# A four-layer attention and expert kernel: constants ahead of the last sends, first rows rounded in halves, the dense expert by 512 columns

## What is computed

```python
topv, topi = jax.lax.top_k(logits, TOP_K)
rank = jnp.cumsum(mask.reshape(TOP_K * N, N_EXP), axis=0).reshape(TOP_K, N, N_EXP) - 1
mask = mask * (rank < capacity)
h = jax.nn.gelu(jnp.einsum('ecd,edh->ech', exp_batches, c_fc), approximate=False)
exp_out = jnp.einsum('ech,ehd->ecd', h, c_proj)
out = jnp.einsum('nec,ecd->nd', cb, exp_out)
```

## Time and profile before

| | |
|---|---|
| three runs | 573.92, 574.77, 574.93 us |
| median | 574.77 us |
| the profiled execution | 573.43 us, span 571.6 us |
| busy, share of the span | PE 85%, PE weight loads 68%, DVE 57%, ACT 42%, POOL 42% |
| instructions | 9125 |
| granted TensorE clock, mean | 0.901 |

### The profile page before, as it was taken

One profiled execution on the slowest core, in us unless ns is written; L12 is line 12 of the kernel. 1 busy time (PEld: TensorE's weight loads), 2 busy tenths in 40 slices (PEclk: granted clock), 3 DMA queues, 4 the chain that ended last, 5 costly groups with the idle time before them and its releaser, 6 DMA issues.

```text
span 571.6 us, 9125 instructions
## 1 busy us (share of the span) xinstructions
PE 483.7 (85%) x3256; PEld 388.0 (68%) x3256; DVE 325.1 (57%) x1137; ACT 238.7 (42%) x473; POOL 241.6 (42%) x350
## 2 busy tenths in 40 slices
PE   2799894779869986995495599999899899999997
PEld 2558383769556625683385399998553788899997
DVE  4866427844996832778751155643776944433334
ACT  2653744324246541444650054421644395334340
POOL 5781866455326011277777525663760340000000
PEclk9799997559758997996599699999999999999999
DMA  9999720311860056800111212114500000000002
GB/s 275 334 205 208 216 99 1 110 34 36 274 193 1 1 147 162 245 1 0 34 51 50 79 57 81 45 34 157 149 2 0 2 2 0 1 1 1 1 1 75
DMA packets 56861, 48.04 MB, mean 84 GB/s; under 512 B 6082, under 2 KB 47240, under 8 KB 56688
## 3 DMA queue, kind: packets, MB, share of 16 engines
q1 hardware_dynamic: 53728, 42.06, 26.5%
q0 software_dynamic: 2656, 4.88, 2.7%
q10 hardware_dynamic: 432, 0.52, 0.4%
HBM read 35.21 MB, written 12.82 MB: 84 GB/s over the span
## 4 chain that ended last, share of the span: by engine, by line
PE 61%; DVE 23%; POOL 6%; issue 5%; ACT 2%; DMA 1%; ACTq 0%; POOLq 0%; DVEq 0%
PE ps L1266 10%; PE ps L1204 7%; DVE st L1660 5%; PE ps L1087 4%; PE ps L1089 4%; PE ps L1088 4%; POOL tok L2381 4%; PE ps L835 3%; PE ps L775 3%; PE ps L722 2%; PE ps L765 2%; DVE mv L1663 2%; PE ps L858 2%; PE ps L838 2%; DVE mx L1698 2%
## 5 line engine op out<-in xcount | busy, mean ns | idle before, releaser
L2113 DVE SCALAR_TENSOR_TENSOR x<-ps,gate,x 128x128 f32<-128x128 f32 x128 | 36.0, 344 | 54.8 <-PE ps L1266 54.8
L1266 PEld LDWEIGHTS ps<-moe_w,big 128*128 128x128 f32 x512 | 61.1, 192 | 3.9 <-issue 1.7
L1538 ACT ACTIVATE big<-ps,col 128x512 f32<-128x512 f32 x64 | 42.2, 689 | 48.2 <-PE ps L1089 48.1
L1266 PE MATMUL ps<-moe_w,big 128*128 128x128 f32 x512 | 61.4, 275 | 0.9 <-DVE x L2102 0.9
L2472 POOL DMA_INDIRECT res<-qT,dest x43 | 42.5, 988 | 40.7 <-DVE qT L2088 25.6
L722 PE MATMUL ps<-con,xn 128*128 128x128 f32 x148 | 28.6, 326 | 28.8 <-ACT xn L1474 15.4
L1530 ACT ACTIVATE big<-ps 128x320 f32<-128x320 f32 x56 | 24.0, 439 | 56.7 <-PE ps L1089 56.6
L722 PEld LDWEIGHTS ps<-con,xn 128*128 128x128 f32 x148 | 19.8, 167 | 39.2 <-DVE xn L1678 35.8
L1204 PE MATMUL ps<-moe_w,big 128*128 128x128 f32 x344 | 41.1, 275 | 0.6 <-ACT big L1530 0.6
L2271 POOL TENSOR_SCALAR rstd<-mv 128x4 f32<-128x4 f32 (+1 forms) x35 | 9.0, 258 | 76.8 <-DVE mv L1663 75.8
L1204 PEld LDWEIGHTS ps<-moe_w,big 128*128 128x128 f32 x344 | 39.8, 192 | 0.8 <-ACT big L1530 0.8
(11 more groups left out here) (353 smaller groups left out, 1179.7 us busy)
## 6 DMA issues: line engine op xcount, KB each, us to landing
ring<-in_ew SPq DMA_DIRECT2D x20, 256.0 KB, 4.8
moe_w<-in_m0w SPq DMA_DIRECT2D x16, 256.0 KB, 6.3
moe_w<-in_m2w SPq DMA_DIRECT2D x16, 256.0 KB, 5.6
tok<-zero SPq DMA_DIRECT2D x1, 2580.0 KB, 27.6
big<-tok SPq DMA_DIRECT2D x7, 322.5 KB, 2.9
res<-zero SPq DMA_DIRECT2D x1, 2048.0 KB, 29.1
moe_w<-in_ew SPq DMA_DIRECT2D x8, 256.0 KB, 5.6
big<-res SPq DMA_DIRECT2D x4, 512.0 KB, 5.0
```

Source lines behind the costliest of these rows:

```text
L1266: last = mm(ps[7 - i % 2 if i >= B else 6 + i % 2][:, cols(c)], big[:, FC * (e % 2) + f, i % B, cols(c)], w[:, e, F + P * f:F + P * f + P] ...
L1538: A(big[:, 2 * (e % 2) + f, t, :], bank[:, :], ACT.Gelu, bias=V("m3b1", 2 * e + f)).then_inc(h_act, 1)
L2113: last = v.scalar_tensor_tensor(out=x[:, C * t + c, :], in0=bank[:, cols(c)], scalar=gate[:, C * t + c, e:e + 1], in1=x[:, C * t + c, :], ...
```

## The change

- First mixture: four constants behind the first four folding products, and three behind all of them.
- `count_second`: DVE first sums the 16 chunks of first choices (`oh_sum`), and one product takes the place of sixteen.
- Dense expert: the hidden layer is made in float32, one product of 512 columns instead of three on rounded operands; POOL no longer splits expert 0, ACT no longer writes `qTR` for this, DVE no longer the remainder. `results_by_dim` makes the result of sequences 0 to 2 with dimensions on partitions, four products of 512 columns. `whole_turned` transposes them back (12 blocks) behind the preparation of the next keys, and DVE adds them to `x` from PSUM (`whole_add`) ahead of the placed experts. Sequence 3 keeps its results by token.
- The last two of the 32 sends count on a semaphore of their own, `sent_last`. PE waits for the other 30, runs nine constants, waits for the last two, and runs ten.
- First placed expert (i = 0): the rows go as 256 and 384 columns. Two transposed blocks go to bank 0 and three to bank 1. DVE rounds the first 256, ACT the other 384, DVE writes both remainders and signals each; the return addresses come after. Four more constants stand behind the transposes. The hidden products of this expert are of 256 and 384 columns.
- Four of the diagonal matrices move from `xT` to `kr_w`. The semaphore `minus_half` becomes a third count on `zeroed`.

```diff
+LAST = 2
+SENT = 16 * (2 * B * C - LAST + 2)
+SENT_LAST = 16 * (LAST + 2)
...
                 if name == "m2":
                     sp.wait_ge(sent, SENT)
+                    sp.wait_ge(sent_last, SENT_LAST)
...
                 last.then_inc(f_mm, 1)
+                keep_busy(ps[3], 4)
                 pe.wait_ge(f_sb, 1)
...
-                for c in range(nb):
-                    mm(ps[1][:, 0:(nb + 1) * E], ones[:, :], bc(oh[:, c, :], [P, nb + 1, E], [1]), start=c == 0, stop=False)
                 pe.wait_ge(oh_ready, 2 * B + 1)
+                mm(ps[1][:, 0:(nb + 1) * E], ones[:, :], bc(oh_sum[:, :], [P, nb + 1, E], [1]), start=True, stop=False)
...
-                        product(ps[2 + f][:, :], w1_high["m2"][:, 0, cols(f)], w1_low["m2"][:, 0, cols(f)],
-                                qTR[:, t, :], whole_low[:, t % 2, :])
+                        elif f % 2:
+                            pe.wait_ge(xT_ready, turns(rows, (f + 1) // 2))
+                        mm(ps[2 + f][:, :], moe_w[:, 0, cols(f)], xT[:, t, :], start=True, stop=True).then_inc(h_mm, 1)
...
+                    for f in range(4):
+                        last = mm(ps[6 + t % 2][:, :], moe_w[:, 0, 512 + P * f:512 + P * f + P], hid[:, t % 2, f, 0:S],
+                                  start=f == 0, stop=f == 3)
+                    last.then_inc(gy_mm, 1)
...
+            def whole_turned():
+                for t in range(B - 1):
+                    pe.wait_ge(gy_sb, done0["whole"] + min(t + 2, B - 1))
+                    if t >= 2:
+                        pe.wait_ge(whole_added, t - 1)
+                    for c in range(C):
+                        last = nc.tensor.transpose(ps[7 - t % 2][:, cols(c)], whole_y[:, C * t + c, :], ident)
+                    last.then_inc(whole_tok, 1)
...
                     fold_weights()
+                    keep_busy(ps[3], 3)
...
                 if name == "m2":
+                    whole_turned()
                     pe.wait_ge(sent, SENT)
-                    keep_busy(ps[7], BUSY // 2 + 2)
+                    keep_busy(ps[2], BUSY // 2 + 2)
+                    pe.wait_ge(sent_last, SENT_LAST)
+                    keep_busy(ps[2], BUSY // 2 + 3)
...
                 turn_group(0)
+                if name == "m2":
+                    keep_busy(ps[2], 4)
                 units = hidden(0)
...
+                if name == "m2":
+                    act.wait_ge(gT_m, PLACED["m0"]["groups"] + 1)
+                    A(xg_high[:, 0, FIRST:], ps[1][:, 0:a["cap"] - FIRST], ACT.Identity).then_inc(first_high, 1)
...
+            def whole_add(t):
+                dve.wait_ge(whole_tok, t + 1)
+                for c in range(C * t, C * t + C):
+                    i = v.scalar_tensor_tensor(out=x[:, c, :], in0=ps[7 - t % 2][:, cols(c - C * t)], scalar=have[:, c:c + 1], in1=x[:, c, :],
+                                               op0=ALU.mult, op1=ALU.add)
+                i.then_inc(whole_added, 1)
...
+                    if name == "m2" and g == 0:
+                        link(v.tensor_copy(xg_high[:, 0, 0:FIRST], ps[0][:, 0:FIRST]))
+                        v.tensor_tensor(xg_low[:, 0, 0:FIRST], ps[0][:, 0:FIRST], xg_high[:, 0, 0:FIRST].bitcast(F32), ALU.subtract).then_inc(gT_s, 1)
+                        dve.wait_ge(first_high, 1)
+                        v.tensor_tensor(xg_low[:, 0, FIRST:], ps[1][:, 0:a["cap"] - FIRST], xg_high[:, 0, FIRST:].bitcast(F32), ALU.subtract).then_inc(gT_s, 1)
```

More of the change, by code:

```diff
@@ L1093, in whole_expert @@
                 pe.wait_ge(loaded, 32 * E)
-                pe.wait_ge(split, 8)
-                pe.wait_ge(x_high, B)
+                rows = n["turn"] - 1
                 def hidden(t):
-                    pe.wait_ge(low_ready, t + 1)
+                    if not late:
+                        pe.wait_ge(xT_ready, turns(rows, t))
                     for f in range(4):
@@ L1119, in whole_expert @@
                 if late:
-                    results(B - 1, hidden(B - 1))
+                    results_by_token(B - 1, hidden(B - 1))
                     return
@@ L2174, in _ @@
             second_largest(False)
+            with_sum = oh[:, 0:nb, :].rearrange("p c e -> p e c")
+            with nc.allow_low_precision(reason="whole numbers up to 16"):
+                v.tensor_reduce(oh_sum[:, :], with_sum, AX.X, ALU.add)
             first_largest(lg2[:, :, :], oh[:, nb:2 * nb, :], slice(0, nb))
```

91 lines of the change are left out of this document (48 added, 43 removed).

## The result

The changed kernel takes **571.73 us** (median of 17 runs, 570.52 to 574.78), the kernel before, run beside it, 574.93 us (median of 17, 573.06 to 577.95). The ratio is 0.9949, with a 95% interval of 0.9935 to 0.9964: 2.9 us faster by the ratio, 3.2 by the medians. In two more sets the unaltered changed kernel came to 0.9937 (0.9918 to 0.9957; medians 571.29 against 575.11 us) and 0.9944 (0.9922 to 0.9967; 571.91 against 575.31). By the three ratios the gain is 2.9 to 3.6 us, by the medians 3.2 to 3.8.

A forecast was written before the change was run, and what follows sets the result against it. PE, 61% of the chain, was taken to bound the kernel, waiting on POOL's sends and DVE's rounding. -4.1 + 0.7 - 0.5 = -3.9 us from 573.43 gave 569.5, as a median 570.9 us; range 569.0 to 573.4.

The forecast's parts named there:

- the three parts: Second mixture 4.1 us faster, late sequence 0.7 us slower, first mixture 0.5 us faster; in sum -3.9 us.
- The dense expert fits under the sends: Second mixture: PE finishes the float32 dense expert at 315.5, the other 30 sends release it at 315.8; no cost, no gain.
- if the clock is low there: Nineteen constants from 315.8: at low clock it rises after some 3.9 us, at 319.7, and they end at 321.9.
- The constants: Second mixture, around the last sends: transposes begin at 321.4, not 322.14; the better clock gives 1.7 of the 4.1 us.
- The halves: First placed expert, second mixture: first product at 322.95, not 325.34, 2.4 us earlier; second half waits 0.2 us.
- the third group's transposes begin at 327.8: Second mixture: they begin there, not at 331.93, with DVE rounding the second group in 2.3 us; part gives 4.1 us.
- The late sequence: Its hidden layer becomes four products of 0.88 us, 3.52 us in all: +0.7 us, bounds 0 and 0.9.
- The first mixture: Constants raise the clock from about 121 us, but the third group's gather limits the gain to 0.5 us; bounds -0.7 and +1.3.
- From the execution to the median: The profiled execution before was 1.3 us faster than the median, 574.77, so 569.5 became a median of 570.9 us.
- The clock falls again in the first mixture: Rival: PE waiting for the gather loses its clock, making the part +1.2 instead of -0.5: 572.6 us; chance 0.24.
- The clock rises late: Rival, second mixture: PE idles a little before the constants, the part gives 2.3 us: 572.7 us; chance 0.10.
- The constants only stand in the way: Slower rival: constants don't raise the clock soon enough, second mixture gains 0: 576.8 us; chance 0.08 for the slower rivals together.

The follow-up runs named there:

- e5: Kernel before with only the split sends' signal, the second mixture's 9 + 10 + 4 constants and first rows in halves; old dense expert kept: 573.46 us, ratio 0.9967.
- e3: Changed kernel with nine constants behind all sends and none behind the first group's transposes, as before the change: 572.16 us, ratio 0.9957.
- e6: Changed kernel without any constants in the second mixture, the first mixture's kept: 573.34 us, ratio 0.9979.
- e4: Changed kernel with the first rows rounded whole by DVE, not in halves, all constants kept: 572.99 us, ratio 0.9977.
- e7: Changed kernel with the late sequence's hidden layer as twelve rounded products again, the three early sequences in float32: 573.69 us, ratio 0.9982.
- e10: Changed kernel with the late sequence's hidden layer in rounded parts and DVE's addresses made ahead of the rounding: 572.15 us, ratio 0.9948.
- e9: Changed kernel unaltered, measured a third time as the base of its set: 571.91 us, ratio 0.9944 to the kernel before.
- e1: Changed kernel unaltered, measured again as the base of its set: 571.29 us, ratio 0.9937 to the kernel before.

## Why the prediction was right, step by step

The median was forecast at 570.9 us and is 571.73, with "faster" as the likeliest case. The steps of the three parts came as forecast, and their sum was 0.4 us too good: 3.9 forecast, 3.5 found. Two things in the account were not right: the float32 dense expert was filed as neither cost nor gain, and the pace of the sends was taken to stay.

- **The dense expert fits under the sends.** Forecast: PE free 0.5 us before the last send begins, release 0.2 us before it. Found: PE free 0.8 before (318.11), release 0.24 before, a wait of 0.58. For the low clock at the start I had added 1.6 us. It was 0.50 until 294 us, and the first sixteen records took 8.42 us in place of 7.04, 1.4 us more. "Costs nothing now" was said of the work that POOL, ACT and DVE drop; but in the traces with the float32 dense expert throughout the sends take 0.3 us less, a gain that the sum lacks. What I had filed as "no gain" was one: e5 shows the transposes 1.3 us later if PE comes to the constants from a pause. The forecast had this as "if the clock is low there" and took six microseconds for the nineteen; they took 6.99, since the clock rose after 5.6 us of constants and not after 3.9 as in the earlier trace rows.
- **The constants.** Forecast transposes at +5.4; found +5.32 to +5.38. PE waits 0.73 to 0.79 us for the load behind the constants, so the load sets that point. That the constants have to stand ahead of the last sends was the smaller part of it: with nine behind all sends (e3) it is 0.3 us less, without any (e6) 2.4 us.
- **The halves.** Forecast first product at +6.96; found +7.10. The wait for the second half that I had put at 0.2 us isn't there: DVE's remainder of the 384 columns ended as the first product of 256 did. e4 puts the halves at 1.25 us. With e6 that covers the part, counted from the changed kernel: 1.25 for the halves and 2.41 for all constants are 3.66 of 3.69 us. No run puts either into the kernel before by itself.
- **The step that was mis-sized** is "the third group's transposes begin at 327.8", +11.8; it was +12.25. I took DVE's rounding of the second group as 2.3 us from the end of its transposes. Its instructions do take 2.28 us (DVE of the changed kernel):

```profile
328.75 0.69 DVE L2096 CAST bigR<-ps 128x512 fp32r<-128x512 f32 x1 [1.97 <-PE ps L1193]
...
330.86 0.17 DVE L2105 TENSOR_TENSOR dest<-dest_f,big 128x5 uint32<-128x5 f32 x1
```

  but the next products start at 328.47, DVE begins at 328.75, and PE takes up the third group 0.15 us after DVE's end: 2.7 us from PE to PE. The way from engine to engine and back was left out. That is 0.3 of the 0.45 us, and the later first product is the rest. The part gave 3.7 us, not 4.1, inside its bounds of 2.3 and 4.6.
- **The late sequence**: forecast +0.7, found +0.63 in the trace, and undone between the same points in e7.
- **The first mixture**: forecast -0.5, found -0.41, and -0.36 in the mean of eleven traces. That the gather is the late one next was right. The first of the two points that I took was not: the transposes begin 5.95 us behind the first folding, not 5.67, since the clock rose as the second foldings ended; the wait of 1.31 us for the gather swallows it.
- **From the execution to the median.** I used the distance of 1.3 us between the profiled execution of before and the median of three runs. Over the sets the median of before is 574.59 to 575.31 us, so this step was between 0.5 us short and 0.2 us too long. In the set of the result it was 0.2 us short, and the medians there differ by 3.2 us, not by 3.9. These two make the 0.8 us between 570.9 and 571.7.
- **The rivals.** *The clock falls again in the first mixture*: not in the profiled execution, where the row of 128 to 129 us has PE at 0.00 busy and the clock at 1.00, but in one of the eleven traces with this code, that of e10. There the part is +1.4 us to the fourth group (16.24 against 14.87 us), close to the rival's +1.2. So the mechanism of the rival is real, and the forecast of the part holds for the executions in which it stays away. The rule that I had cited for it, from the Trainium skill, "TensorE: Matmul & The Clock Gate", Part 4: PE-mode transpose (transposes don't hold the clock as products do), is neither borne out nor refuted here: two groups of transposes lay in that time in all eleven, with eight products (sixteen records) beside them, and the clock fell in one. *The clock rises late*: not in the change, where it never fell between 295 and 332 us, but it is what happened in e5. *The constants only stand in the way*: e5 is the mild form of it, 1.3 us, and shows the condition, a PE that comes from a long pause (7.36 us). Even so its third group comes at +13.48 and that of e6, without any constants in the second mixture, at +14.69.

## What to carry to other kernels

Products of constants around a wait pay most if the engine reaches them with its clock up, or if they end before the awaited data lands. Otherwise a part of them is work on the path: 1.3 us in e5, whose third group still came 1.2 us ahead of that of e6, which has none (but another dense expert). A wait that one trace passes at full clock isn't safe in the next (e10). Where one engine rounds or copies for another, cut the first piece small, signal it before anything the consumer doesn't read, and count the way there and back, some 0.3 us and 0.15 us here, beside the instructions. And read a part's worth between two points of one trace: here these repeat to 0.1 us, while whole executions of one kernel spread over 4 us. But put the points far enough apart. Counting from the last send hid 0.3 us in the sends, and ending at the third group hid the fallen clock of e10.

## What was not expected of the hardware

- **How long the clock took to come back differed widely for the same products.** The same 512-column products of constants, started at 0.50, brought it up after 3.9 us in the kernel before, about 3 us in e3 and 5.6 us in e5. In e6, where products and a pause alternated, it took 7 us. A forecast that takes one of these as the duration can be off by several microseconds.
- **The clock outlasts a pause for a while.** In e3 it was still 1.00 up to 317 us, with PE busy for 0.63 of 4 us, and 0.52 in the next. The pauses of 0.4 to 0.9 us around the last sends of the changed kernel didn't lower it, nor did those of 1.31 and 1.70 us in the first mixture of the changed kernel and of e9; in e10 it fell with one of 1.42 us.
- **It can fall without a pause of PE.** In e1 the clock stood at 1.00 from 430 to 444 us and at 0.53 from 444 to 446, and the trace has PE busy throughout (2.00 of 2 us from 444 to 446, as in the stretches ahead of it). What PE ran from 440.94 to 444.92 us were 32 records of products of 36 columns (L866). Whether these brought it down, no run shows.
- **The start of a kernel scatters more than the change moves.** The first folding began between 116.54 and 118.87 us in fourteen traces, and the last send between 315.35 and 318.93, in code that hardly differs. The kernel before happened to be early (116.76 and 315.99). The stretch between the two points takes 197.5 to 200.8 us (199.2 in before), so no single trace could have shown the 3.5 us in its span.
